# Reordering the head of a fused transformer block: first mixing ahead of the second x1, transposes inside the K product, one offset step moved to GpSimd

## The reference, cut to what matters

```
h  = layernorm(x) * (1 + ca) + sa
u, gate = split(h @ W_in.T)                      # 256 and 256 channels
b_t  = u @ W_state.T ;  dt = min(softplus(u @ W_dt.T + b_dt), 10)
decay = exp(-dt * (softplus(A_log) + 1e-4))
state[t] = decay[t]*state[t-1] + (1-decay[t])*b_t[t]      # scan over the 512 tokens
x1 = x + ga * (((state @ W_C.T) * silu(gate) + h * D) @ W_out.T)
h2 = layernorm(x1) * (1 + cb) + sb ;  p = h2 shifted by one token
xk = mu_k*h2 + (1-mu_k)*p ;  xr = mu_r*h2 + (1-mu_r)*p
out = x1 + gb * sigmoid(xr @ W_r.T) * (relu(xk @ W_k.T)**2 @ W_v.T)
```

## Time and profile before

| | us |
|---|---|
| median of 3 runs | 347.96 (346.74 to 348.77) |
| the profiled execution, its device time | 347.26 |
| its span in the profile | 345.5 |
| PE busy | 336.7 (97%) |
| DVE busy | 305.2 (88%) |
| ACT busy | 294.2 (85%) |
| POOL busy | 274.5 (79%) |

### The profile page before, as it was taken

The page is one execution under the profiler, slowest core; times in us unless marked ns, Lnnn a source line. Parts: engine busy times, 40 slices in busy tenths (PEclk is TensorE's granted clock), DMA queues, the critical chain, the costliest instruction groups (busy, mean ns, idle before and its releaser), DMA issues.

```text
span 345.5 us, 5204 instructions
## 1 busy us (share of the span) xinstructions
PE 336.7 (97%) x1576; PEld 266.0 (77%) x1576; DVE 305.2 (88%) x463; ACT 294.2 (85%) x396; POOL 274.5 (79%) x273
## 2 busy tenths in 40 slices
PE   8999989799999999999999999999999999999995
PEld 4666657588888888888888888888888888887764
DVE  3789869999999999999999999999999989887846
ACT  4576777999899998989899999989899899888484
POOL 2251849989899898989899898989999896966742
PEclk9999999999999999999999999999999999999999
DMA  8950523051421505151340605142230601010013
GB/s 290 418 201 11 171 89 97 1 183 61 142 104 55 190 1 185 62 184 62 104 139 22 225 2 183 63 182 63 74 109 3 183 3 61 0 64 0 0 64 121
DMA packets 18556, 36.00 MB, mean 104 GB/s; under 512 B 4960, under 2 KB 5728, under 8 KB 18400
## 3 DMA queue, kind: packets, MB, share of 16 engines
q1 hardware_dynamic: 17808, 35.19, 29.3%
q10 hardware_dynamic: 720, 0.48, 0.4%
HBM read 27.22 MB, written 8.44 MB: 103 GB/s over the span
## 4 chain that ended last, share of the span: by engine, by line
PE 82%; DVE 8%; issue 4%; ACT 4%; POOL 2%; DVEq 0%; POOLq 0%; ACTq 0%
PE slot L292 67%; PE slot L385 4%; PE slot L299 3%; PE slot L536 2%; PE slot L526 2%; PE slot L527 2%; PE slot L313 1%; ACT prev L662 1%; DVE xn L919 1%; PE slot L393 1%; DVE xn L930 1%; DVE h L925 1%; POOL rstd L1166 1%; PE slot L332 0%; PE slot L306 0%
## 5 line engine op out<-in xcount | busy, mean ns | idle before, releaser
L1156 POOL TENSOR_TENSOR k_lo<-k_act,k_hi 128x512 fp32r<-128x512 f32 x30 | 51.5, 1735 | 4.5 <-ACT k_act L864 4.5
L662 ACT ACTIVATE prev<-slot,mod,mix_prev 128x512 f32<-128x512 f32 x64 | 46.4, 783 | 0.9 <-PE slot L592 0.6
L1156 POOL TENSOR_TENSOR xk_lo<-xk,xk_hi 128x512 fp32r<-128x512 f32 x30 | 38.5, 1307 | 7.9 <-ACT xk_hi L700 7.9
L292 PE MATMUL slot<-h_hi,wf_hi 128*128 128x512 f32 x120 | 43.4, 402 | 0.8 <-DVE z L994 0.8
L1156 POOL TENSOR_TENSOR xr_lo<-xr,xr_hi 128x512 fp32r<-128x512 f32 x32 | 42.1, 1320 | 0.2 <-ACT xr_hi L706 0.2
L292 PE MATMUL slot<-h_hi,wf_lo 128*128 128x512 f32 x120 | 42.0, 390 | 0.0
L1212 POOL TENSOR_TENSOR h_lo<-h,h_hi 128x512 fp32r<-128x512 f32 x28 | 36.4, 1301 | 2.4 <-ACT h_hi L681 2.4
L1266 POOL TENSOR_TENSOR z_lo<-z,z_hi 128x512 fp32r<-128x512 f32 x26 | 33.3, 1302 | 2.8 <-ACT z_hi L850 2.8
L292 PE MATMUL slot<-h_lo,wf_hi 128*128 128x512 f32 x120 | 34.2, 390 | 0.0
L964 DVE SCALAR_TENSOR_TENSOR xk<-slot,mix_new,prev 128x512 f32<-128x512 f32 x32 | 23.8, 746 | 8.0 <-issue 5.6
L930 DVE TENSOR_SCALAR xn<-slot,stats,rstd 128x256 f32<-128x256 f32 x62 | 29.2, 532 | 0.0
(11 more groups left out here) (161 smaller groups left out, 982.8 us busy)
## 6 DMA issues: line engine op xcount, KB each, us to landing
x_ch<-x_ch_in SPq DMA_DIRECT2D x16, 512.0 KB, 4.3
x_tok<-x_tok_in SPq DMA_DIRECT2D x15, 512.0 KB, 5.6
x_out<-wmod SPq DMA_DIRECT2D x15, 512.0 KB, 3.2
spread_rows<-rows_spread SPq DMA_DIRECT2D x13, 512.0 KB, 3.8
wmod<-wmod_in SPq DMA_DIRECT2D x1, 1024.0 KB, 8.6
w_in<-weights_in SPq DMA_DIRECT2D x1, 1024.0 KB, 11.3
w_in<-weights_in SPq DMA_DIRECT2D x1, 512.0 KB, 4.5
wmod<-wmod_in SPq DMA_DIRECT2D x1, 512.0 KB, 5.8
```

Of the source, the lines that this page charges most:

```text
L292: ins = nc.tensor.matmul(out, w[:, c, at + d * P:at + (d + 1) * P], x[:, c, :], start=first, stop=last)
L662: return nc.scalar.activation(prev[:, mix, i, 1:T + 1], ps_n[:, i, :], ACT.Identity, bias=mod_at(SHIFT2 + i, k), scale=mix_prev[:, mix, i, ...
L1156: nc.gpsimd.tensor_tensor(lo, x, hi.bitcast(F32), ALU.subtract).then_inc(done, 1)
```

## The change

It reorders the head and the first step of the loop:

- VectorE mixes both halves of batch 0 ahead of `after_attention(1)`, and does `scaled(3)` ahead of them instead of after `normalised(1)`.
- TensorE transposes `x1` of batch 1 inside the K product of batch 0, and the wait ahead of K is for `xk` of the second half alone.
- The offsets of batch 3 are made by GpSimd (`first_offsets`), at the end of its head, instead of by ScalarE ahead of `previous`.
- ScalarE loads the silu table after `rounded_h(2)` instead of ahead of `modulated(2, ...)`; it makes the roundings of `xk` and `xr` of batch 0 together, ahead of `exponential(2)`; it does the Relu of batch 0 ahead of `rounded_state(2)`, and `rounded_h(3)` and then the table load ahead of the first Tanh instead of loading the table ahead of `rounded_state(2)` and rounding after the Tanh. `rounded_h(3)` waits for `b_ps` in addition.
- For batch 0's first norm ScalarE takes one token tile and VectorE three, in a form that needs no shift; VectorE makes the negated mean. VectorE's copy of `w_front` goes behind the first modulation. Two of the four `keep_warm` matmuls are gone.

```
@@ tensor
-            keep_warm(slot[3][:, 0, :], 4)
+            keep_warm(slot[3][:, 0, :], 2)
...
-            token_stats(1)
...
-                    for done in (*xk_ok, *xr_ok):
-                        pe.wait_ge(done, d + 1)
+                    pe.wait_ge(xk_ok[1], d + 1)
                     half(k_out, wl_hi, MIX_K, xk_hi, 0, first=True)
                     half(k_out, wl_lo, MIX_K, xk_hi, 0)
+                    if d == 0:
+                        token_stats(c)
@@ scalar
-                for t in range(TT // 2):
+                for t in range(TT // 2 if k > 0 else 1):
...
+                if k == WHOLE + 1:
+                    act.wait_ge(b_ps, k)
                 nc.scalar.copy(h_hi[:], h[:, k % 2]).then_inc(hhi_ok, 1)
...
             decays(1)
-            nc.scalar.preload_act_table_set("silu_and_others")
             ...
             modulated(2, 1).then_inc(h_ok, 1)
             rounded_h(2)
+            nc.scalar.preload_act_table_set("silu_and_others")
             gate_silu(1)
...
-            offsets(WHOLE + 1)
...
             rounded_xk(0, 0)
+            rounded_xr(0, 0)
+            rounded_xr(0, 1)
+            rounded_xk(0, 1)
             exponential(2)
-            rounded_xk(0, 1)
-            rounded_xr(0, 0)
             decays(2)
-            rounded_xr(0, 1)
-            nc.scalar.preload_act_table_set("silu_and_others")
+            rectified(0)
             rounded_state(2)
...
+                if d == 0:
+                    rounded_h(a)
+                    nc.scalar.preload_act_table_set("silu_and_others")
                 if live(d) and c < LAST:
                     gate(d)
@@ vector
+            dve.wait_ge(mv1_ok, 1)
+            nc.vector.tensor_scalar(spread1[:, 0, 0, :], mv1[:, 0, :, 0], -1.0, None, ALU.mult).then_inc(minus1_ok, 1)
...
-            ln1_apply(0)
-            dve.wait_ge(front_ps, 1)
-            nc.vector.tensor_copy(w_front[:], slot[1][:, :, 0:2 * NS]).then_inc(front_ok, 1)
+            ln1_first()        # waits for rstd1; tiles 1 to 3: (x_tok - mean) * rstd
             dve.wait_ge(mod1_ps, 1)
             ...
+            dve.wait_ge(front_ps, 1)
+            nc.vector.tensor_copy(w_front[:], slot[1][:, :, 0:2 * NS]).then_inc(front_ok, 1)
...
             ln1_rows(4)
+            scaled(WHOLE + 1)
             mixing(0, 0)
+            mixing(0, 1)
             after_attention(1)
-            mixing(0, 1)
             clipped(2)
             after_transpose(1)
             driven(2)
             scanned(2)
             normalised(1)
-            scaled(WHOLE + 1)
             modulated(WHOLE + 1)
@@ gpsimd
+            def first_offsets(k):
+                pool.wait_ge(s_row_in[k % 2], 16 * ((k - WHOLE + 1) // 2))
+                pool.wait_ge(root_ok, 1)
+                for i in range(CH):
+                    last = nc.gpsimd.tensor_scalar(offset1[:, i], spread_rows[:, k % 2, SHIFT], scale_neg[:, i, k:k + 1],
+                                                   mod_at(SHIFT1 + i, k), ALU.mult, ALU.add)
+                last.then_inc(offset_ok, 1)
...
             ln1_rows(WHOLE + 2)
+            first_offsets(WHOLE + 1)
```

More of the change, by code:

```diff
@@ L201, in adaln_block @@
         scaled1_ok = sem("scaled1_ok")
+        minus1_ok = sem("minus1_ok")
         spread1_ok, slo_ok, rstd1_ok, shift1_ok, rstd2_ok, first_ok = sem("spread1_ok"), sem("slo_ok"), sem("rstd1_ok"), sem("shift1_ok"), sem("rstd2_ok"), sem("first_ok")
@@ L716, in gate_silu, with rectified @@
                 nc.scalar.activation(silu[:], ps_gate(k)[:], ACT.Silu).then_inc(silu_ok, 1)
+            def rectified(k):
+                act.wait_ge(k_ps, k + 1)
+                before(act, klo_ok[0], k)
+                before(act, klo_ok[1], k)
+                nc.scalar.activation(k_act[:], ps_k(k)[:], ACT.Relu).then_inc(relu_ok, 1)
             ln1_apply(0)
@@ L783, in _ @@
                     exponential(b)
[L784 to L788, removed]
+                if 0 < d < LAST:
+                    rectified(d)
                 if live(b):
@@ L837, in _ @@
                     act.dma_start(out_d[d, P:, quarter[1]], x2[:, d % 2, 1, quarter[1]]).then_inc(s_out[d % 2], 16)
-                if live(a) and a > WHOLE:
+                if live(a) and a > WHOLE + 1:
                     rounded_h(a)
@@ L901, in ln1_apply, with ln1_first @@
                     last = nc.vector.tensor_scalar(xn1[:, t, :], x_tok[:, k % 3, t, :], rstd1[:, k % 2, t:t + 1], shift1[:, k % 2, t:t + 1], ALU.mult, ALU.add)
+                last.then_inc(xn1b_ok, 1)
+            def ln1_first():
+                dve.wait_ge(rstd1_ok, 1)
+                for t in range(1, TT):
+                    last = nc.vector.tensor_scalar(xn1[:, t, :], x_tok[:, 0, t, :], mv1[:, 0, t, 0:1], rstd1[:, 0, t:t + 1], ALU.subtract, ALU.mult)
                 last.then_inc(xn1b_ok, 1)
@@ L1162, in ln1_scale @@
                 before(pool, xn1b_ok, k - 1)
-                nc.gpsimd.tensor_scalar(spread1[:, k % 2, 0, :], mv1[:, k % 2, :, 0], -1.0, None, ALU.mult)
+                if k > 0:
+                    nc.gpsimd.tensor_scalar(spread1[:, k % 2, 0, :], mv1[:, k % 2, :, 0], -1.0, None, ALU.mult)
                 nc.gpsimd.tensor_scalar(spread1[:, k % 2, 1, :], mv1[:, k % 2, :, 1], EPS, None, ALU.add).then_inc(spread1_ok, 1)
@@ L1167, in ln1_scale @@
                 pool.wait_ge(rstd1_ok, k + 1)
+                if k == 0:
+                    pool.wait_ge(minus1_ok, 1)
                 nc.gpsimd.tensor_tensor(shift1[:, k % 2], spread1[:, k % 2, 0, :], rstd1[:, k % 2], ALU.mult).then_inc(shift1_ok, 1)
@@ L1212, in low_h @@
                 nc.gpsimd.tensor_tensor(h_lo[:, i], h[:, k % 2, i], h_hi[:, i].bitcast(F32), ALU.subtract).then_inc(hlo_ok[i], 1)
+            def first_offsets(k):
+                pool.wait_ge(s_row_in[k % 2], 16 * ((k - WHOLE + 1) // 2))
+                pool.wait_ge(root_ok, 1)
+                for i in range(CH):
+                    last = nc.gpsimd.tensor_scalar(offset1[:, i], spread_rows[:, k % 2, SHIFT], scale_neg[:, i, k:k + 1], mod_at(SHIFT1 + i, k), ALU.mult, ALU.add)
+                last.then_inc(offset_ok, 1)
             ln1_scale(0)
```

## The result

The changed kernel takes 343.69 us (median of 4, 343.59 to 344.21) against 347.75 for the kernel before (median of 4): ratio 0.9873, 95% interval 0.984 to 0.9906. The profiled execution takes 343.59, its span is 341.8, so 3.7 of the 4.1 are in the two profiles.

A forecast was written before the change was run, and what follows sets the result against it. TensorE's own work was taken to bound the kernel from K(1) on, head waits limiting the gain to 3.7 us. K(1) moving from 67.36 to 64.96 gains 2.4: profiled 347.26 becomes 344.9, median 345.6; range 344.3 to 347.2.

The forecast's parts named there:

- What bounds the kernel, and the bound on the gain: TensorE's own work fills the time from K(1) on, unchanged; head waits of 3.51 us plus warm-up bound the gain: 3.7.
- Start: Until 34 us: two fewer warm-up matmuls gain 0.15 us (bounds 0 and 0.3); the later w_front copy is hidden.
- The first wait: token_stats(0) on TensorE, 0.40 us late for h of batch 2: moving the table load behind the rounding removes the 0.40.
- The 0.2 that the gate product was said to have left: With the table load moved, the Silu begins as now and the gate product needing the load has some 0.2 us left.
- K(1): The first K product of batch 1 on TensorE; forecast to start at 64.96 us instead of 67.36.
- First mixing: Batch 0's mixing: prev starts at 42.85 instead of 44.20; scaled(3) fills VectorE's wait, taking 1.40 us if undisturbed.
- GpSimd's offsets: Batch 3's offsets at the end of GpSimd's head: 1.4 us each taken, bounds 0.3 and 2.0; hidden at that value.
- the rival that ended slower: GpSimd's offsets far dearer: gain gone at 3.0 us each, at 4.0 the kernel 2 us slower, 350.0; chance 0.06.
- From the scan to K(1): h of batch 3 ready at 56.1, prev of batch 1 at 59.3, K(1) at 64.96; ScalarE late; gain 2.4 us.
- The wait for the rounded `z`: On TensorE ahead of K(1): takes the place of the shrinking k_lo wait; rounded z comes behind two prev, at 61.3.
- The collision at `modulated(3)`: Rival: GpSimd starts xr_lo just before VectorE's addition, which starts 0.9 us later; gain 1.5, time 346.5; chance 0.12.
- From the profile to the median: Profiled execution of 347.26 becomes 344.9 us; it lay 0.7 under the median of 347.96, so the median becomes 345.6.

The follow-up runs named there:

- e1: The kernel before with one edit: K waits for the second xk alone instead of both xk and both xr; 346.65 us, ratio 0.9969.
- e2: The kernel before with all four waits ahead of K kept but reordered xr, xr, xk, xk, so the last-met stands last; 346.99 us, ratio 0.998.
- e3: The changed kernel with the four waits ahead of K restored; 344.97 us.
- e7: The changed kernel with the silu table loaded ahead of h of batch 2 again, as before; 344.54 us.
- e10: The changed kernel with scaled(3) moved behind normalised(1) again; 347.85 us.
- e3 to e8: Changed kernel with one part undone each: K waits, warm-up matmuls, offsets, x1 order, first load, h(3) rounding; 344.97, 344.14, 345.26, 344.60, 344.54, 344.36 us.
- e11: The kernel before with K waiting for the second xk alone, run again beside the version with filled waits; 346.54 us.

## Why the prediction was right in part, and where it failed

**What bounds the kernel, and the bound on the gain: wrong.** "The change leaves that work alone" and later "In the loop nothing changes" are the step that failed. A TensorE that is busy for 19.63 of 19.63 us was read as one that does nothing but its own work. Two waits, already met, behind the one met last took 0.08 of each step, and the profile books that as busy time. The change takes them out: the steps lose 0.85 us in ten, and e1, e2 and e3 put it on these waits (0.79, 0.80 and 0.72). The limit of 3.7 us, made of the waits of the head alone, lacked this too. The diff had the edit in plain sight; it was told and priced at nothing, without naming what hides it.

**Start: not contradicted.** 0.15 was forecast for the warm-up matmuls; 0.11 lies between the two profiles and 0.1 at the most in the mean of all, within the spread of one kernel. The times behind the start came as forecast, so the copy of `w_front` cost nothing there; it was not tested by itself. The profiles differ by 0.34 more in the start of the modulation. This is chance: the changed kernel again started it at 7.94, as the kernel before did at 7.96.

**The first wait: right in kind, low in size.** 0.40 forecast; the head is 0.56 longer without it (e7). The 0.2 that the gate product was said to have left was not there: it waits for the Silu, and TensorE loses 0.35 up to 38.68. The transposes of `xn2` come 0.61 earlier all the same (41.35 + 0.34 against 42.30), so K(1) doesn't feel it.

**First mixing: right.** With the start's 0.34 taken off, `prev` of batch 0 was forecast at 42.85 and came at 42.51 + 0.34 = 42.85; `scaled(3)` took the 1.40 chosen.

**GpSimd's offsets: mis-sized, without effect.** 1.4 each taken, 0.78 measured (1.55 for the two). The upper bound of 2.0, from the slope of narrow operations, was far off. The Trainium skill (GPSIMD Engine Reference, "Engine selection") was nearer with one-input work at about line rate: the estimate from it was 0.65. The measured 0.78 also rules out the rival that ended slower.

**From the scan to K(1): the times right, one wait elsewhere.** `h` of batch 3 forecast at 56.1, at 55.69 + 0.34 = 56.03; `prev` of batch 1 at 59.3, 59.35; K(1) at 64.96, 64.93. As forecast, ScalarE was what is late. The wait for the rounded `z` that was forecast did not come: TensorE goes on to it at 61.10 without a pause. It had been held up before by two waits of 0.5 for `xr_lo`, which the forecast didn't have. K(1) doesn't feel which of the two it is, as ScalarE's chain sets it.

**The collision at `modulated(3)`: the rival's mechanism is real, its case did not come.** `state_lo` runs from 53.32 to 54.61, the addition that starts at 54.15 ends at 55.69, and `xr_lo`, started at 54.56, takes 2.27 and ends at 56.83: its own 1.3 begins about when the addition ends. The Trainium skill (SBUF — State Buffer, "SBUF: two separate sides") has the rule that who comes first holds the shared ports for the whole instruction, and these rows agree. The addition came ahead of `xr_lo`, so GpSimd paid most. With `scaled(3)` late (e10) both pay: VectorE's two take 2.71 and 2.13, and GpSimd's `k_lo` 3.96 instead of 2.56.

**From the profile to the median: incomplete.** I took the difference of the two medians to be that of the profiles, so the 0.7 by which the profiled execution lay under its median was carried over. The changed kernel's profiled execution lies only 0.1 under its median. Of the 1.9 us between 345.6 and 343.69, this is 0.6; the other 1.3 lie between the profiled executions, 344.9 and 343.59. In 30 of 76 executions the kernel before runs at a lower mean clock and takes 0.6 to 3.4 us more than the median of the others, the changed one and its variants e3 to e8 in none of 39. Of the executions at full clock the median of before is 347.29, so 3.6 of the 4.1 us stand against the changed kernel's 343.69; on the one chip where both were run with their clocks on record it is 347.17 against 344.02, or 3.2. The profiled execution, at a clock of 0.999, could not show what the waits near 61 and 63 us cost beyond their length.

In sum, of the profiles' 3.7: 2.3 from the head and 0.1 from the warm-up matmuls, together the 2.4 of the forecast; 0.85 from the loop's waits, which was missed; 0.34 from the start, by chance. The 0.4 from the profiles to the medians is of the size of the clock's part and of the spread of the starts together; the runs do not part these two further.

## What to carry to other kernels

An engine that is shown busy all the time may still be waiting. Look at the instruction that waits for several semaphores: if one of them is met last each time and only just in time, put it last, or drop those that it implies. Count idle time in a TensorE-bound head more than once: besides its length it can cost the clock in some executions, so look at the granted clock of every run, not only of the profiled one. And undo an edit only with its partners: an order on one engine (here the mixings) may be worth something only because of an order on another (the roundings ahead of the exponential).

## What the runs showed of the hardware that was not expected

- Two waits that are met already cost TensorE 0.08 us together when they stand behind the one met last (19.63 against 19.55 a step, e1 to e3), and nothing measurable ahead of it (e2). The profile shows no idle time for it.
- Two waits of 0.9 and 0.8 us within 3 us, at the end of a stretch with full clock, were followed by matmuls at half rate for some 3 us in the first experiment's profile, 1.5 us lost; in the profiles of the kernel before and of e2 and e11 the same waits passed at full clock. A low mean clock came in four of ten executions of such kernels. With six matmuls of zeros in the waits, 1.3 us of TensorE's idle time, it came in 2 of 23, at no cost to the schedule (55.85 against 55.86).
- GpSimd does a tensor_scalar of 128x512 with two per-partition scalars in 0.78 us, where its two-input operations of that size take 1.30.
